# Random-feature attention: features computed by slices of 32 channels, in units of four heads

## The reference

```python
def favorplus_features(x, proj, eps=1e-6):           # x: (B, h, T, 8), proj: (h, 32, 8)
    xw = einsum('bhtd,hmd->bhtm', x, proj)
    xw = xw - max(xw, axis=-1, keepdims=True)
    return exp(xw) * exp(-0.5 * sum(x * x, -1)) + eps
Q, K, V = heads(Wq), heads(Wk), heads(Wv)            # of layernorm(x)
phiQ = favorplus_features(Q / sqrt(8), proj);  phiK = favorplus_features(K / sqrt(8), proj)
KV, Ksum = einsum('bhtm,bhtd->bhmd', phiK, V), sum(phiK, axis=2)
out = einsum('bhtm,bhmd->bhtd', phiQ, KV) / (einsum('bhtm,bhm->bht', phiQ, Ksum) + 1e-6)
x = x + out @ Wo.T + bo
```

## Time and profile before

| | us |
|---|---|
| median of 3 runs | 1267.42 |
| the runs | 1258.23, 1267.42, 1267.85 |
| the profiled execution | 1264.36 |
| its span, first to last instruction | 1262.5 |
| mean granted TensorE clock in it | 0.87 of full |
| busy: PE, DVE, ACT, POOL | 1031.8, 845.8, 382.9, 270.5 |
| stage 2, from DVE's first unit to the last residual | 433.5 to 561.5 |

### The profile page before, as it was taken

How to read it: one execution, slowest core, us unless ns; L and a number is a source line. 1 busy time by engine, 2 the same in 40 slices (tenths; PEclk the granted TensorE clock), 3 DMA queues, 4 the chain that set the end, 5 groups by cost and what they waited for, 6 DMA issues and landing times.

```text
span 1262.5 us, 16374 instructions
## 1 busy us (share of the span) xinstructions
PE 1031.8 (82%) x6027; PEld 638.2 (51%) x6027; DVE 845.8 (67%) x2101; ACT 382.9 (30%) x622; POOL 270.5 (21%) x231
## 2 busy tenths in 40 slices
PE   4898988989989788899978872899999566898465
PEld 2254555543434466683333331667768344676344
DVE  5676657756565586656777547548556896688896
ACT  1154444533333233223332225312211122231121
POOL 3600000003222211001222210310210243333232
PEclk8698888989989997759998986899999896787786
DMA  8623030020000000000000000000000000000000
GB/s 237 156 102 77 2 77 2 3 87 1 1 1 0 1 1 1 1 2 0 1 1 0 1 0 3 1 1 1 1 1 1 0 1 1 2 2 2 1 9 25
DMA packets 9948, 25.35 MB, mean 20 GB/s; under 512 B 979, under 2 KB 7315, under 8 KB 9171
## 3 DMA queue, kind: packets, MB, share of 16 engines
q1 hardware_dynamic: 9568, 23.44, 6.6%
q10 hardware_dynamic: 294, 0.79, 0.3%
HBM read 16.69 MB, written 7.34 MB: 19 GB/s over the span
## 4 chain that ended last, share of the span: by engine, by line
PE 53%; DVE 32%; issue 6%; ACT 3%; POOL 3%; DMA 2%; SPq 0%; DVEq 0%; ACTq 0%; POOLq 0%
PE ps L686 5%; DVE a_MN L359 4%; PE ps L673 4%; PE ps L678 3%; PE ps L252 3%; DVE XN L117 2%; DVE q_E L1252 2%; DMA a_QS<-a_MT 2%; POOL rs L96 2%; PE ps L194 2%; PE ps L1513 2%; PE ps L214 2%; PE ps L1467 2%; PE ps L1510 2%; PE ps L2043 2%
## 5 line engine op out<-in xcount | busy, mean ns | idle before, releaser
L359 DVE TENSOR_REDUCE a_MN<-ps 128x1 f32<-128x384 f32 (+3 forms) x176 | 107.6, 638 | 64.3 <-PE ps L197 62.0
L96 POOL TENSOR_TENSOR rs<-t,mhalf 128x4 f32<-128x4 f32 x37 | 37.4, 1010 | 409.4 <-DVE t L90 409.3
L930 POOL TENSOR_TENSOR f_Y<-f_Y,f_TT 128x512 f32<-128x512 f32 x56 | 70.9, 1266 | 178.5 <-DVE f_TT L820 178.5
L465 ACT ACTIVATE a_PT<-ps 128x1024 f32<-128x1024 f32 x64 | 65.1, 1025 | 72.4 <-PE ps L218 71.3
L143 DVE TENSOR_TENSOR X<-ps,X 128x512 f32<-128x512 f32 x32 | 22.0, 688 | 96.1 <-PE ps L1523 49.4
L895 ACT ACTIVATE f_HH<-ps,pack_zero 128x512 f32<-128x512 f32 x64 | 44.0, 687 | 132.8 <-PE ps L673 132.8
L194 PE MATMUL ps<-a_KS,a_QS 72*128 72x128 bf16 (+3 forms) x256 | 70.9, 339 | 13.6 <-DVE a_MN L359 10.4
L686 PE MATMUL ps<-f_HH,pack_zero 128*128 128x512 f32 x128 | 74.0, 661 | 5.7 <-DVE f_TT L820 5.7
L811 DVE TENSOR_TENSOR f_XS<-ps,XNT 128x512 f32<-128x512 f32 x64 | 43.9, 688 | 46.8 <-PE ps L666 46.8
L673 PE MATMUL ps<-f_XS,pack_zero 128*128 128x512 f32 x128 | 68.5, 618 | 1.3 <-DVE f_XS L811 1.3
L820 DVE SCALAR_TENSOR_TENSOR f_TT<-ps,pack_zero,f_X 128x512 f32<-128x512 f32 x64 | 47.9, 748 | 32.2 <-PE ps L686 32.2
(11 more groups left out here) (306 smaller groups left out, 2364.9 us busy)
## 6 DMA issues: line engine op xcount, KB each, us to landing
scratch<-a_parts SPq DMA_DIRECT2D x16, 384.0 KB, 4.3
a_QS<-scratch SPq DMA_DIRECT2D x3, 1152.0 KB
a_KS<-scratch SPq DMA_DIRECT2D x9, 384.0 KB
pack_one<-in_one SPq DMA_DIRECT2D x1, 2679.5 KB, 9.4
pack_zero<-in_zero SPq DMA_DIRECT2D x1, 2607.5 KB, 16.2
a_QS<-scratch SPq DMA_DIRECT2D x4, 288.0 KB
a_KS<-scratch SPq DMA_DIRECT2D x12, 96.0 KB
X<-in_x SPq DMA_DIRECT2D x4, 256.0 KB, 10.0
```

What stands on the lines that cost most here:

```text
L96: pool.tensor_tensor(M.rs[:, 4 * b:4 * b + 4], M.t1[:, 4 * b:4 * b + 4], M.mhalf[:, 0:4], ALU.pow).then_inc(root.sem, root.tick(n, b))
L359: dve.tensor_reduce(M.a_MN[:, n % 2, ti, h0:h0 + k], bank(M, M.bank["a_max", n, jj], 128 * (ti + 1) * k).rearrange("p (a c) -> p a c", a=k ...
L465: act.activation(M.a_PT[:, c % 6, 0:1024], M.ps[:, a * 512:a * 512 + 1024], ACT.Exp).then_inc(made.sem, made.tick(n, hh))
L930: pool.tensor_tensor(M.f_Y[:, i, :], M.f_Y[:, i, :], M.f_TT[:, u % 3, :], ALU.add).then_inc(made.sem, made.tick(n, u))
```

## The change

A unit becomes all 512 tokens of a slice of four heads (32 channels), g = 0..3, instead of 128 tokens of all heads. Its features are four matmuls of 32 rows and 128 columns, one per tile of tokens, into bank 2 + g. The slices are computed in interleaved pairs, (0, 1) ahead of the half-batch's steps and (2, 3) after two of them. The squares' sums are no longer made per unit: one `squares` on PE per half-batch makes four matmuls into bank 7, and ACT copies them, halved, to the new tile `p_HF` (`halves`); DVE adds from there. The 1e-6 for keys is added by POOL (`keys`), and the one for queries is the bias of ACT's copy of the transposed queries. `p_XW` has four buffers instead of three; `heads` has one bank (6) instead of two; a `turn_tensor` in the queries' half moves from bank 4 to bank 7. POOL's order changes: the root of batch b - 1 comes at the end of its batch b, not behind the squares of batch b + 1.

```diff
@@ attn_b_tensor
-    def features(b, w, j):
...
-        take(pe, M, 2 + c % 3)
...
-        pe.matmul(bank(M, 2 + c % 3), M.p_QT[:, i, tk], M.p_proj[:, :], start=True, stop=True)
...
-        pe.matmul(bank(M, 5 + c % 2, H), M.p_SQ[:, i, tk], M.sel_h[:, :], start=True, stop=True).then_inc(made.sem, made.tick(c))
...
+    def squares(b, w):
+        i, made = "kq".index(w), S["p_sqs"]
+        take(pe, M, 7)
+        pe.wait_ge(S["p_sq"].sem, S["p_sq"].at(b, w))
+        for j in range(4):
+            m = pe.matmul(bank(M, 7, H, 16 * j), M.p_SQ[:, i, 128 * j:128 * j + 128], M.sel_h[:, :], start=True, stop=True)
+        m.then_inc(made.sem, made.tick(b, w))
+        M.freed[7] = (S["p_half"], (b, w))
+
+    def features(b, w, pair):
+
         i, made = "kq".index(w), S["p_feat"]
+        for g in pair:
+            take(pe, M, 2 + g)
+        pe.wait_ge(S["p_qt"].sem, S["p_qt"].at(b, w))
+        for j in range(4):
+            for g in pair:
+                row = slice(32 * g, 32 * g + 32)
+                m = pe.matmul(bank(M, 2 + g, 128, 128 * j), M.p_QT[row, i, 128 * j:128 * j + 128], M.p_proj[row, 128 * g:128 * g + 128],
+                              start=True, stop=True, skip_group_check=True)
+                if j == 3:
+                    m.then_inc(made.sem, made.tick(8 * b + 4 * i + g))
+        for g in pair:
+            M.freed[2 + g] = (S["p_dxw"], (8 * b + 4 * i + g,))
...
@@ attn_b_tensor, the loop
+        for w in "kq":
+            features(b, w, (0, 1))
+            squares(b, w)
+            if w == "k":
                 project(b, "q")
                 if b == 2:
                     turn_tensor(pe, S, M, 2, 3, 7, M.XN, (S["normed"], (2, 3)))
...
+            elif b + 1 < 4:
                 project(b + 1, "k")
...
+            for j in range(4):
+                if j == 2:
+                    features(b, w, (2, 3))
+                step(b - 1, 4 * "kq".index(w) + j)
+                if w == "q" and j == 1 and b >= 2:
+                    turn_tensor(pe, S, M, 3, b - 2, 7, M.XN, (S["normed"], (3, b - 2)))
+            if w == "k":
+                values(b)
         sums(b)
@@ attn_b_vector, subtract
...
         dve.tensor_reduce(MX, xw, AXX, ALU.max).then_inc(v.sem, v.tick())
+        if g == 0:
+            dve.wait_ge(S["p_half"].sem, S["p_half"].at(b, w))
         dve.wait_ge(v.sem, v.n)
-        dve.scalar_tensor_tensor(MX, bank(M, 5 + c % 2, H), 0.5, MX, ALU.mult, ALU.add).then_inc(mx.sem, mx.tick(c))
...
+        dve.tensor_tensor(MX4, MX4, sq, ALU.add).then_inc(mx.sem, mx.tick(c))
...
-    def add(b, w, j):
...
-        dve.tensor_scalar((M.p_PK, M.p_PQ)[i][:, b % 2, j, :], M.p_XW[:, c % 3, :], 1e-6, None, ALU.add).then_inc(phi.sem, phi.tick(c))
@@ attn_b_scalar
+    def halves(b, w):
+        i, made = "kq".index(w), S["p_half"]
+        if b:
+            act.wait_ge(S["p_mx"].sem, S["p_mx"].at(8 * b + 4 * i - 5))
+        act.wait_ge(S["p_sqs"].sem, S["p_sqs"].at(b, w))
+        act.activation(M.p_HF[:, i, :], bank(M, 7, 64), ACT.Copy, scale=0.5).then_inc(made.sem, made.tick(b, w))
...
-        act.activation(M.p_PT[:, c % 3, :, :], bank(M, c % 2).rearrange("p (g t) -> p g t", g=4), ACT.Copy).then_inc(made.sem, made.tick(c))
+        act.activation(M.p_PT[:, c % 3, :, :], bank(M, c % 2).rearrange("p (g t) -> p g t", g=4), ACT.Identity, bias=M.p_eps[:, 0:1]).then_inc(made.sem, made.tick(c))
...
         values(b)
+        halves(b, "q")
@@ attn_b_gpsimd
+    def keys(b, g):
+        if g == 0 and b >= 2:
+            pool.wait_ge(S["p_kv"].sem, S["p_kv"].at(b - 2))
+        pool.wait_ge(S["p_exp"].sem, S["p_exp"].at(8 * b + g))
+        pool.tensor_scalar(M.p_PK[:, b % 2, g, :], M.p_XW[:, g, :], 1e-6, None, ALU.add).then_inc(phi.sem, phi.tick(b, g))
...
+        for g in range(4):
+            if g == 1:
+                squares(b, "q")
+            keys(b, g)
+        if b + 1 < 4:
+            squares(b + 1, "k")
...
+        if b:
+            norm_root(pool, S, M, 3, b - 1)
```

More of the change, by code:

```diff
@@ L980, in sums @@
         pe.wait_ge(S["p_va"].sem, S["p_va"].at(b))
[L981 removed]
+        pe.wait_ge(S["p_phi"].sem, S["p_phi"].at(b, 3))
         for g in range(4):
             for j in range(4):
[L984 removed]
+                m = pe.matmul(bank(M, 7, 33, 33 * g), M.p_PK[:, i, g, 128 * j:128 * j + 128], M.p_VA[:, 4 * b + j, g, :],
                               start=(j == 0), stop=(j == 3))
@@ L991, in queries @@
         take(pe, M, c % 2)
-        pe.wait_ge(S["p_phi"].sem, S["p_phi"].at(8 * b + 4 + j))
+        if j == 0:
+            pe.wait_ge(S["p_exp"].sem, S["p_exp"].at(8 * b + 7))
         for g in range(4):
-            pe.transpose(bank(M, c % 2, 128, 128 * g), M.p_PQ[:, b % 2, j, 128 * g:128 * g + 128], M.ident[:, :]).then_inc(made.sem, made.tick(c))
+            pe.transpose(bank(M, c % 2, 128, 128 * g), M.p_PQ[:, b % 2, g, 128 * j:128 * j + 128], M.ident[:, :]).then_inc(made.sem, made.tick(c))
         M.freed[c % 2] = (S["p_pt"], (c,))
     def heads(b, j):
-        c, made, bk = 4 * b + j, S["p_heads"], 5 + (4 * b + j) % 2
-        take(pe, M, bk)
+        c, made = 4 * b + j, S["p_heads"]
+        take(pe, M, 6)
         pe.wait_ge(S["p_pt"].sem, S["p_pt"].at(c))
@@ L1003, in heads @@
         for g in range(4):
-            m = pe.matmul(bank(M, bk, 36, 36 * g), M.p_PT[:, c % 3, g, :], M.p_KV[:, b % 2, g, :], start=True, stop=True)
+            m = pe.matmul(bank(M, 6, 36, 36 * g), M.p_PT[:, c % 3, g, :], M.p_KV[:, b % 2, g, :], start=True, stop=True)
         m.then_inc(made.sem, made.tick(c))
-        M.freed[bk] = (S["p_on"], (c,))
+        M.freed[6] = (S["p_on"], (c,))
     def turned(b):
@@ L1151, in project, with exp @@
         act.activation(M.p_QT[:, i, :], bank(M, i), ACT.Copy, scale=float(8 ** -0.5)).then_inc(made.sem, made.tick(b, w))
-    def exp(b, w, j):
-        c, made = 8 * b + 4 * "kq".index(w) + j, S["p_exp"]
+    def halves(b, w):
[4 more added lines that the diff above has]
+        act.activation(M.p_HF[:, i, :], bank(M, 7, 64), ACT.Copy, scale=0.5).then_inc(made.sem, made.tick(b, w))
+    def exp(b, w, g):
+        c, made = 8 * b + 4 * "kq".index(w) + g, S["p_exp"]
+        if w == "q" and g == 0 and b >= 2:
+            act.wait_ge(S["p_qturn"].sem, S["p_qturn"].at(4 * (b - 2) + 3))
         act.wait_ge(S["p_dxw"].sem, S["p_dxw"].at(c))
-        act.activation(M.p_XW[:, c % 3, :], M.p_XW[:, c % 3, :], ACT.Exp).then_inc(made.sem, made.tick(c))
+        out = M.p_XW[:, c % 4, :] if w == "k" else M.p_PQ[:, b % 2, g, :]
+        act.activation(out, M.p_XW[:, c % 4, :], ACT.Exp).then_inc(made.sem, made.tick(c))
     def values(b):
@@ L1187, in attn_b_scalar @@
     for b in range(4):
+        halves(b, "k")
         for j in range(4):
@@ L1209, in attn_b_gpsimd, with squares @@
 def attn_b_gpsimd(pool, S, M):
-    ones, sq, xb = S["p_ones"], S["p_sq"], S["p_xb"]
-    pool.memset(M.p_VA[:, :, :, 32:33], 1.0).then_inc(ones.sem, ones.tick())
-    for b in range(4):
[L1213 to L1224, removed]
+    ones, sq, xb, phi = S["p_ones"], S["p_sq"], S["p_xb"], S["p_phi"]
+    def squares(b, w):
+        i = "kq".index(w)
+        if b:
+            pool.wait_ge(S["p_sqs"].sem, S["p_sqs"].at(b - 1, w))
+        pool.wait_ge(S["p_qt"].sem, S["p_qt"].at(b, w))
+        pool.tensor_tensor(M.p_SQ[:, i, :], M.p_QT[:, i, :], M.p_QT[:, i, :], ALU.mult).then_inc(sq.sem, sq.tick(b, w))
+    def keys(b, g):
[3 more added lines that the diff above has]
+        pool.tensor_scalar(M.p_PK[:, b % 2, g, :], M.p_XW[:, g, :], 1e-6, None, ALU.add).then_inc(phi.sem, phi.tick(b, g))
+    pool.memset(M.p_VA[:, :, :, 32:33], 1.0).then_inc(ones.sem, ones.tick(0))
+    pool.memset(M.p_eps[:, :], 1e-6).then_inc(ones.sem, ones.tick(1))
+    squares(0, "k")
+    for b in range(4):
+        for g in range(4):
[4 more added lines that the diff above has]
+            squares(b + 1, "k")
+        pool.wait_ge(S["normed"].sem, S["normed"].at(2, b))
+        pool.tensor_tensor(M.X[:, 4 * b:4 * b + 4, :], M.X[:, 4 * b:4 * b + 4, :],
+                           M.p_bo[:, :].unsqueeze(1).to_broadcast([128, 4, 128]), ALU.add).then_inc(xb.sem, xb.tick(b))
+        if b:
+            norm_root(pool, S, M, 3, b - 1)
     norm_root(pool, S, M, 3, 3)
```

52 lines of the change are left out of this document (14 added, 38 removed).

## The result

The changed kernel takes 1288.3 us, the median of five runs (1286.2 to 1296.3), against 1266.96 us of before on the same chip (five runs, 1258.2 to 1267.9). The ratio is 1.0186 with a 95% interval of 1.0157 to 1.0216: slower by about 21 us on the medians. The profiled execution took 1296.26 us, the slowest of the five by 8 us, with a span 31.9 us longer than that of before.

A forecast was written before the change was run, and what follows sets the result against it. DVE bound batches 0 and 1, PE at a lowered clock batches 2 and 3. Low-clock batches of 131.3 against 113.4 us, tail +1.5 and lifts -3 gave +16 on 1264.4, 1280.4, forecast as 1282; eight-in-ten range 1250 to 1292.

The forecast's parts named there:

- The +16 net: Whole stage and tail: +17.9 for batches at low clock, +1.5 for the tail, -3 for short returns of the clock.
- the walk: All four queues stepped through at low clock: batches 0 to 3 at 19.8, 36, 39 and 36.5 us.
- 3 us off behind the walk: Dense stretch lifts the clock in two of three batches, some 5 us each, returning 1.5 us each.
- a standstill of 3.5 us: Batch 0: PE stands until the values' copy near 440.9, so the clock drops to 1.2 GHz from about 440.
- rival A: Clock stays full through the stage, 93.8 instead of 113.4 us, tail nearer 10 than 15: 1240 us; chance 0.13.
- Wait (1): Query squares need bank 7 from ACT's values copy; 2.6 us from the last key unit's end through halving.
- (2): Query slices 2 and 3 stand behind `turned`, which waits for DVE's last division, itself behind unit 0; no separate size.
- (3): Batches 2 and 3: `turn_tensor` shares bank 7, waits for exp and ACT's copy, delaying slices 2 and 3: 2.2 us each.
- the bounds 0.54 to 2.2: POOL's 512-column key add, bounded in us from its 128x128 row and four times that; expected to cost nothing.
- -16.2 us of DVE: The 1e-6 adds leaving DVE: 32 x 0.507 us, a unit becoming 1.53 us instead of 2.04.
- the 7.8 us: POOL's new order removes three waits of DVE for the root at `norm_back`: -7.8 us.
- The walk at full clock: All four queues stepped through at full clock: batches 15.0, 25.0, 27.3 and 26.5 us, 93.8 in sum.

The follow-up runs named there:

- e3_sqown: Changed kernel with the query squares in bank 0 and ACT halving them before copying the values: 1295.7 us, ratio 1.0265 to before.
- e8_fullrows: Changed kernel with each feature matmul reading all 128 rows instead of its slice's 32, same result and order: 1278.9 us, ratio 1.0081 to before.
- e7_all: Changed kernel plus unread 512-column matmuls on PE, query squares in bank 0, turn_tensor later in bank 2: 1269.6 us, ratio 1.0012 to before.
- e9_full_mended: Changed kernel with 128-row features, query squares in bank 0 and turn_tensor later in bank 2: 1270.3 us, ratio 1.0027 to before.
- e5_adds: Kernel before with POOL's new order, key adds on POOL, query bias on ACT, four p_XW buffers; units, features, squares unchanged: 1249.1 us, again 1245.4.
- e4_root: Kernel before with only POOL's root moved ahead of the query square: 1250.1 us, ratio 0.9896 to before.
- e4_again: Kernel before with only POOL's root moved ahead of the query square, timed again on another chip: 1253.1 us, ratio 0.9902 to before.
- e6_sqown_turn: Changed kernel with query squares in bank 0, halved before the values' copy, and turn_tensor moved to step 3, bank 2: 1293.1 us, ratio 1.0167.

## Why the prediction was right, point by point

**The decision was the clock, and it went as forecast.** The stage's clock is 0.54, and the median lies 6 us above the forecast, in its range and on its side. Batch 1 at low clock was walked at 36 us and took 36.4, but that agreement is partly luck: 7 us of it ran at full clock, and e3_sqown, where it did not, took 40.4. The +16 net stands against +21 measured on the medians (+26.6 in the stage of the profiled execution, the slowest of its five).

**The sizes that were off.** All the low-clock durations taken from rows at other places were a little short. The sums were put at 6.2 us and take 7.03, a pair of slices 1.55 and 2.01, the squares 1.55 and 1.82 to 1.89. The pairs adjoin their neighbours in the chain without a gap, as in the retention stage; what makes a pair 0.46 us longer here was not tested. Per batch that is one sum, four pairs and two squares: 0.8 + 4 x 0.46 + 2 x 0.3 = 3.2 us if all lay in the path. The batches came out 1.7, 0.4, 2.2 and 2.7 us above the walk, 7.0 in sum. The measured batches hold the three lifts already (about 7, 3.4 and 3.4 us), for which the forecast's sum took 3 us off behind the walk; so the walk itself was short by some 10 us.

**The place and the cause of the first fall were wrong.** It was to come near 440, behind a standstill of 3.5 us. It came at about 434, out of the sparse stretch before, where PE had one pair of 32-row matmuls and 1.03 us of squares around 1.62 us of idle time. e8_fullrows bears on this step: it has the standstill, 2.37 us long, and stays at 1.00. What went before the fall in the changed kernel is thin work with gaps, in four traces of four, and the standstill was no part of it. That the forecast came out right in spite of this is luck: the low clock came from another cause, and earlier; rival A (full clock if no standstill) would have been ruled out for a wrong reason. e3_sqown takes the wait away and stays at 0.52.

**The new waits.** Wait (1) exists: DVE stood 2.26 us for the halving in batch 0 (1 to 2 had been forecast), and 11.0 us in seven such waits in all. The halving took 224 ns, 0.2 forecast. Behind wait (1) PE itself stood only 0.80 us, once; behind (2) it stood 2.9 us in three, and behind (3) 3.1 us in two, the longer 1.6, where 2.2 each had been forecast. Mending (1) and (3) seems worth 7 to 9 us where the clock is up (e7_all, e9_full_mended) and nothing measurable where it is low, since PE's own work then fills most of them. The walk at low clock counted 2.6 and 2.2 us in full.

**The part that leaves DVE.** The add on POOL takes 1500 ns, inside the bounds 0.54 to 2.2, and PE never waited for it in the changed kernel (0.2 us in e5_adds); the bias costs 677 against 586 ns, 0.09 as forecast. The two hold nothing back. But -16.2 us of DVE is worth 8 us where it was measured on top of the root, since PE is close behind.

**The root.** Two waits of 3.3 us, in batches 2 and 3, are gone, as predicted. The third of the 7.8 us was misread: it is 1.13 us long, lies ahead of the stage's first unit, behind the stage before, and POOL's new order doesn't touch it; it is still there in the changed kernel and in e4_root. So the term is 6.7 us, not 7.8:

```profile
429.93 0.16 DVE L101 TENSOR_TENSOR t<-rs 128x4 f32<-128x4 f32 x1 [1.13 <-POOL rs L96]
...
481.65 0.16 DVE L101 TENSOR_TENSOR t<-rs 128x4 f32<-128x4 f32 x1 [3.33 <-POOL rs L96]
```

Alone the move is worth 12 to 13 us. What goes beyond the waits fits the clock, which fell in or right behind those waits and stays at 0.96 in e4_root's trace, with a tail of 9.7 us for 14.5. But that execution is the fastest of its seven (1242.4 us, the median 1250.1); in e4_again's trace the clock is 0.85, the tail 14.5 us and the stage 10 us shorter than before. The prediction named that link, and then priced the root by its waits alone; rival A's tail "nearer 10" was right in three of the four traces with the root early and units as before.

**The walk at full clock** was 15.0 us for batch 0 and 25 to 27 for the others. Batch 0 of e8_fullrows, at 1.00 and with the walk's waits, has 16.1, and that of e9_full_mended, at 0.93 and with two of them mended, 14.8; both have more PE work in the features than the walk. Batches 1 to 3 never showed it: e7_all and e9_full_mended take 31 to 36 us there, at mean clocks of the stage of 0.89 and 0.80, with extra PE work in both. What slices would take at full clock without that work stays open, since nothing here kept the clock up without adding work for PE.

## What to carry to other kernels

Before work on PE is made thinner, by tiling rows for one, read the granted clock by stretch: here features 1.6 times as fast (1.14 us for 1.86) went with a stage at 0.54 of the full clock instead of 0.80, and full rows with that much more work were 10 us faster. A wait that stands next to a fall of the clock can be worth more than its length, so a change of order that removes it comes first: one moved root took away 6.7 us of waits and gave 12. Read the clock of more than one execution before explaining a single fall of it: the same kernel had 0.96 and 0.85 in two. And measure the parts of a bundle alone; this one held 19 to 20 us of gain under 42 of loss.

## What the runs showed of the hardware

PE can be busy throughout and be granted 1.2 GHz: 18.00 of 18 us at 0.50 in e3_sqown, 20.20 of 21 at 0.50 in batch 0 of the changed kernel, with 32-row slices, 16-column squares, 33-column sums and 36-column products, and the projections and transposes between them. Wide matmuls at the same places raised it from 0.53 to 0.86. The Trainium skill (TensorE: Matmul & The Clock Gate, Part 1) has the clock follow how busy PE has been recently; these rows agree only if busy there is not what the profile counts as busy.

The Trainium skill (TensorEngine Tiling (Array Packing), When to Use Tiling) recommends row tiling for a contraction of 32. The engine's own time agrees, 1.14 us for a pair against 1.86, but the kernel's does not (1288.3 against 1278.9 us).

The same program can be granted different clocks: e4_root and e4_again, on two chips, did the same work for 12.9 us and were then granted 1.00 and 0.50, and e6_sqown_turn got 6.6 us at 1.00 in a batch where e3_sqown, in the same order, stayed at 0.50, again on another chip.

A POOL `tensor_scalar` add of 128x512 f32 takes 1.50 us, 2.8 times the 0.54 of 128x128.
